# The row maximum of a full attention tile, taken in two parts on VectorE

## The reference, cut to what matters

```python
T, D, H, HD = 1250, 512, 8, 64
# spatial attention (KS_) and cross attention (KC_): every token sees every token
att = softmax(einsum('bthd,bshd->bhts', q, k), axis=-1)     # 1250 x 1250 for each head
o   = einsum('bhts,bshd->bthd', att, v)
# temporal attention (KT_): the same with a causal mask, row t sees columns 0..t
```

## Time and profile before

| | |
|---|---|
| median of 3 runs | 1983.16 us (1981.05 to 1983.17) |
| the profiled execution, its own time | 1988.85 us |
| its span in the profile | 1987.1 us |
| spatial attention, first maximum to last exponential | 516.9 to 821.5 us |
| causal attention | 1033.2 to 1249 us |
| cross attention | 1366.2 to 1671 us |
| busy over the span | PE 87%, DVE 60%, ACT 45%, POOL 35% |

### The profile page before, as it was taken

The page is one execution under the profiler, slowest core; times in us unless marked ns, Lnnn a source line. Parts: engine busy times, 40 slices in busy tenths (PEclk is TensorE's granted clock), DMA queues, the critical chain, the costliest instruction groups (busy, mean ns, idle before and its releaser), DMA issues.

```text
span 1987.1 us, 27321 instructions
## 1 busy us (share of the span) xinstructions
PE 1720.9 (87%) x9816; PEld 1411.9 (71%) x9816; DVE 1186.2 (60%) x2214; ACT 886.9 (45%) x1736; POOL 693.5 (35%) x448
## 2 busy tenths in 40 slices
PE   2776989859999999798977777699999998789998
PEld 1544876548788888676866666577888887568776
DVE  7998124630588888631057777515888886873333
ACT  3774321311477777512145665313777775321000
POOL 4021010033525424022346454135245337253331
PEclk9988999969999999898989999799999999889999
DMA  3000000132021111023311223011121130011111
GB/s 97 7 22 22 0 23 15 57 125 60 19 52 28 27 33 42 6 89 131 73 26 27 52 49 134 17 39 40 31 48 27 27 91 20 12 43 37 37 37 57
DMA packets 33003, 88.42 MB, mean 44 GB/s; under 512 B 5190, under 2 KB 5660, under 8 KB 32369
## 3 DMA queue, kind: packets, MB, share of 16 engines
q1 hardware_dynamic: 32881, 86.83, 16.2%
HBM read 43.29 MB, written 12.80 MB: 28 GB/s over the span
## 4 chain that ended last, share of the span: by engine, by line
PE 53%; DVE 25%; ACT 10%; issue 6%; DMA 2%; SPq 1%; POOL 1%; DVEq 1%; ACTq 0%; POOLq 0%
PE ps L568 10%; PE ps L569 10%; PE ps L570 10%; DVE ngm L1402 7%; PE ps L740 6%; ACT F L933 5%; PE ps L750 4%; PE ps L741 4%; DVE R L1411 4%; PE ps L767 3%; DVE F L1297 3%; ACT R L944 3%; PE ps L689 2%; DVE F L1423 2%; PE ps L786 2%
## 5 line engine op out<-in xcount | busy, mean ns | idle before, releaser
L438 POOL TENSOR_TENSOR w_hi<-w_raw,zero 128x512 fp32r<-128x512 f32 x96 | 109.5, 1141 | 803.2 <-PE ps L570 505.5
L944 ACT ACTIVATE R<-ps 125x500 fp32r<-125x500 f32 (+3 forms) x624 | 278.1, 513 | 243.3 <-PE ps L750 242.5
L1402 DVE TENSOR_REDUCE ngm<-ps 125x1 f32<-125x1250 f32 (+5 forms) x240 | 302.3, 1260 | 60.9 <-PE ps L741 55.9
L1411 DVE TENSOR_TENSOR R<-ps,R 125x500 fp32r<-125x500 f32 (+3 forms) x624 | 326.2, 574 | 17.4 <-ACT R L944 16.8
L740 PE MATMUL ps<-R 128*125 128x512 f32 (+4 forms) x624 | 258.9, 415 | 61.1 <-DVE R L1411 55.1
L933 ACT ACTIVATE F<-ps,ngm 125x1250 f32<-125x1250 f32 (+5 forms) x240 | 277.7, 1157 | 76.1 <-DVE ngm L1402 72.0
L767 PE MATMUL ps<-R 125*128 125x252 f32 (+1 forms) x2080 | 300.2, 289 | 8.7 <-DVE F L1423 7.9
L750 PE MATMUL ps<-ident,F 125*125 125x125 f32 x2040 | 270.9, 278 | 10.7 <-ACT F L933 10.7
L767 PEld LDWEIGHTS ps<-R 125*128 125x128 f32 x2080 | 261.0, 190 | 10.9 <-DVE R L1411 9.4
L750 PEld LDWEIGHTS ps<-ident,F 125*125 125x125 f32 x2040 | 249.6, 192 | 14.9 <-ACT F L933 12.9
L568 PE MATMUL ps<-R,w_hi 128*128 128x512 f32 (+1 forms) x576 | 213.8, 371 | 41.9 <-POOL w_lo L453 13.9
(11 more groups left out here) (172 smaller groups left out, 2478.0 us busy)
## 6 DMA issues: line engine op xcount, KB each, us to landing
R<-F SPq DMA_DIRECT2D x96, 312.5 KB, 5.2
w_raw<-in_weights SPq DMA_DIRECT2D x96, 256.0 KB, 2.7
TB<-in_x SPq DMA_DIRECT2D x10, 250.0 KB
x_d<-F SPq DMA_DIRECT2D x10, 250.0 KB
zt_d<-F SPq DMA_DIRECT2D x1, 2500.0 KB, 8.5
F<-zt_d SPq DMA_DIRECT2D x1, 2500.0 KB, 12.4
qc_d<-F SPq DMA_DIRECT2D x4, 625.0 KB, 3.9
xt_d<-F SPq DMA_DIRECT2D x4, 625.0 KB, 3.4
```

What stands on the lines that cost most here:

```text
L438: return eng.tensor_tensor(to, a, zero[0:to.shape[0], :].to_broadcast(list(to.shape)), ALU.add)
L944: eng.activation(PT[0][:, g % 2, 4 * bank:4 * bank + nb, n % 2, 0:P], ps[0:P, 3 * (n % 2) + bank, 0:P * nb].rearrange("p (c t) -> p c t", ...
L1402: eng.tensor_reduce(out=ngm[0:P, n % 2:n % 2 + 1], in_=flat(n % 2)[0:P, 0:K.cols[i]], op=ALU.max, axis=AX.X, negate=True).then_inc(A.negma ...
L1411: eng.tensor_tensor(PT[1][blk], ps[0:P, 3 * (n % 2) + bank, 0:P * nb].rearrange("p (c t) -> p c t", c=nb), PT[0][blk].bitcast(F32), ALU.su ...
```

## The change

In a full attention tile PE counts a new semaphore `A.early` up when the second bank of scores has landed. DVE then takes the maximum of columns 0 to 1023 as soon as that has come, the maximum of columns 1024 to 1249 when `A.scores` has come, and the smaller of the two negated values with a `tensor_tensor` of one column. Both reduces go through `link`. The causal attention keeps its code.

```diff
+        ngp = sb("ngp", [128, 2, 2])
...
-        A = Sems(sem, "att", "qin0 qin1 cut scores negmax exp tr hi lo pv inv ihi ilo bc bot post norm lk")
+        A = Sems(sem, "att", "qin0 qin1 cut early scores negmax exp tr hi lo pv inv ihi ilo bc bot post norm lk")
...
                     ins = eng.matmul(to, QSL[b][:, P * i:P * i + P], KS[b][:, lo:lo + w], start=False, stop=True)
+                    if c == 1 and not K.causal:
+                        ins.then_inc(A.early, 1)
                 ins.then_inc(A.scores, 1)
...
                 def greatest(c, hp, n):
+                    i = n % NT
+                    if not K.causal:
+                        t = 2 * NT * hp + n + (H * NT if K.turn else 0)
+                        eng.wait_ge(A.early, t + 1)
+                        c(eng.tensor_reduce(out=ngp[0:P, n % 2, 0:1], in_=flat(n % 2)[0:P, 0:1024], op=ALU.max,
+                                            axis=AX.X, negate=True))
+                        eng.wait_ge(A.scores, K.tile(hp, n))
+                        c(eng.tensor_reduce(out=ngp[0:P, n % 2, 1:2], in_=flat(n % 2)[0:P, 1024:T], op=ALU.max,
+                                            axis=AX.X, negate=True))
+                        eng.tensor_tensor(ngm[0:P, n % 2:n % 2 + 1], ngp[0:P, n % 2, 0:1], ngp[0:P, n % 2, 1:2], ALU.min
+                                          ).then_inc(A.negmax, 1)
+                        return
                     eng.wait_ge(A.scores, K.tile(hp, n))
-                    i = n % NT
```

## The result

The changed kernel takes 2074.82 us (median, 2068.95 to 2076.91) beside 1982.59 us before: 1.046 times as long, with a 95% interval of 1.044 to 1.048. The direction was as forecast, the size was not: 92 us instead of 26, far above the range. Its profiled execution has a span of 2075.1 us against 1987.1.

What follows compares the result with a forecast made beforehand. A chain of waits through DVE, PE and ACT, 7.54 us per two tiles, was taken as the bound, not PE. Per stage 9.5 + 3.0 + 0.4 = 12.9 us, for two +26: 1983.16 + 26 = 2009 us, range 1999 to 2025.

Steps and rivals of the forecast that it cites:

- the term of the minimum: One-column minimum after the two reduces on DVE: taken to last 0.15 us, the next instruction starting 0.07 after its start.
- What the split costs: Two reduces, links and minimum in place of one reduce on DVE: +0.38 us to `probs_lo` and to the end of `ngm`.
- The bound below: Least price of the minimum on DVE: not nothing, as no DVE row is under 0.13 us and starts are 0.07 apart.
- The odd tile: Odd-numbered tile's maximum, behind `output` on DVE: on the chain of waits, so each two-tile round takes 0.38 us more.
- The four rounds of a gap: Rounds where `spread_inverses` fills PE, three such stretches a stage: +1.0 us for each stretch, 3.0 us a stage.
- The margin of 0.07 for the even tile: Even tile's `ngm` ready at 571.60, ACT's exponential starting at 571.67: 0.07 us left, so no cost, narrowly.
- The price of a link: Chained DVE instruction starts 0.03 us after the previous end, an unchained one 0.08 before it: 0.11 us for each link.
- The rule that a semaphore costs nothing extra: Skill's rule, weighed and not followed: the split would cost 0.16 us a round, the sum near 9 us instead of 26.
- No change: Rival: PE is the bound after all, its slack absorbing DVE's extra work; time stays 1983 us; 4%.
- faster: Rival: the early start of the even tile's maximum decides; 16 us gained at no split cost, 1967 us; 3%.
- cheap links: Rival: a linked DVE instruction starts like one without a wait; split costs 0.16 us, 1992 us; 8%, up to 2001.
- The even tile comes onto the chain as well: Rival: minimum takes 0.30 us, even tile's `ngm` 0.08 too late, round grows by 0.61, 2026 us; 15% above 2018.

Runs made afterwards that it cites:

- the twin with the reduce: The changed kernel with the minimum of the two partial maxima taken by a tensor_reduce over two columns instead of a tensor_tensor: 2015.13 us, 1.0136 times the kernel before.
- even tiles only: The changed kernel with a tensor_reduce minimum and the split in even-numbered tiles alone, odd tiles keeping one reduce: 1986.45 us, 0.9995 times the kernel before.
- the run without the early start: The changed kernel with a tensor_reduce minimum and both partial reduces waiting for `A.scores`: 2023.61 us, 1.0197 times the kernel before.

## Why the prediction was wrong, and where it was right

**The step that failed** is the term of the minimum in the part "What the split costs": "the nearest is the one-element TENSOR_SCALAR of the router, 0.14 us ... I take 0.15 and 0.07, the row being of the same size", with an upper bound of 0.30 from L1401. It measured 0.525 on average, up to 2.345. I chose the row by size, and what mattered was its operands: the router's instruction has one tensor input, L1401 takes one of its two from PSUM, and the minimum reads two tensors from SBUF, where it waits for the running GpSimd instruction. Nothing in the prediction looked at GpSimd, whose work I had only named as "other queues". (The bound below, "no DVE row is under 0.13", was wrong too: the memsets of L1473 take 0.08. It changed nothing.) The trace of before did show the wait. At 1715 us, in the timeline of both engines, before:

```profile
1715.35 1.03 POOL L557 TENSOR_TENSOR R<-F,zero 128x500 fp32r<-128x500 f32 x1 [2.07 <-ACT F L1110]
1715.41 1.51 DVE L1529 TENSOR_TENSOR F<-F 125x512 f32<-125x512 f32 x1
```

L1529 adds two SBUF tiles of 512 columns; the shortest of its ten takes 0.69 us, this one 1.51, because it gets going only when L557 ends, at 1716.38. The Trainium skill states the rule ("SBUF — State Buffer", section "SBUF: two separate sides"): VectorE and GpSimd share one pair of SBUF ports as an exclusive lock that goes to whoever starts first, for a whole instruction. On VectorE an instruction with two SBUF inputs needs it while GpSimd reads SBUF, and one that runs in a two-port mode needs it too. The runs here agree on two inputs, with up to 2345 ns against at most 158 for the reduce with its one. (That the tensor_scalar of 200 columns ran in a two-port mode no run shows.) They agree on the other direction as well: L557 at 1711.81, behind an L1529 that had started at 1711.70, took 1.46 us instead of 1.03. "For a whole instruction" doesn't fit L487, which let the minimum through 0.77 us after its start of 2.07; there the measurement decides.

**What it added.** Of the 95 us in the two stages, 27 are the split itself (the twin with the reduce: 13.5 + 13.8; forecast 12.9 each). The minima's waits are 84.0 - 24.8 = 59 us. That leaves 9, and the two stages show a granted clock of 0.96 and 0.97 in place of 0.99. Two rounds of the changed kernel, from `output` to `output`, and the stretch of low clock in the second (length, busy time by engine, then the granted clock):

```profile
563.78:573.42 9.64, 7.53 (x54) 6.36 (x53) 8.64 (x13) 5.84 (x11) 8.60 (x4) 1.00 0.01 2
573.42:584.25 10.83, 8.75 (x53) 7.92 (x52) 8.89 (x14) 5.84 (x11) 6.17 (x4) 0.84 0.00 1
579.07:582.49 3.42, 3.42 (x17) 3.31 (x16) 2.65 (x5) 1.41 (x4) 0.97 (x1) 0.50 0.00 0
```

The first is 1.72 us longer than a round with a short minimum (7.92) and holds waits of 0.72 + 1.05 = 1.77 us: the waits pass into the round one to one. The second is 2.90 us longer with 1.83 us of waits (the minimum at 575.43). PE had been idle for 2.08 us up to 578.06, from 579.07 on its clock was at 0.50 (1.2 GHz), and ten transposes took 2.33 us where the usual is 1.26. Over 78 such rounds the waits are 48.9 us and the lengthening over the twin's rounds is 55.1. What lies between is in seven rounds with a granted clock of 0.83 to 0.85 and three right behind one of these (7.4 us together); no other round is more than 0.1 us longer than its waits. The remaining 13 us, 10 of them waits, lie in the first and last tiles of the stages. No run here holds the clock still, so that the low clock is the cause of the rest is read from the place where it lies.

**The rest of the working**, judged by the twin with the reduce, where the failed term is right: 28 us for 26. From the first reduce to `probs_lo` 1.76 for 1.75. Round 7.94 for 7.92, and 8.05 for 8.05 in second heads. The odd tile carries the whole cost and the even tile none: right (even tiles only: 0.9995). The four rounds of a gap are 1.1 us longer (31.15 to 32.25, in the second pair of heads) for 1.0. The margin of 0.07 for the even tile: about right, as the run without the early start shows, since 0.22 later made 0.15 of a round in second heads and 0.18 in first heads. The price of a link, 0.11: 0.12 measured. The rule that a semaphore costs nothing extra (the Trainium skill, "VectorE: DVE Perf Modes", "The DRAIN you can't avoid") doesn't hold for these reduces: 1.26 against 1.14 us from start to start.

**The rivals.** No change and faster fell, and so did cheap links, with 0.12 us for one. "The even tile comes onto the chain as well" came nearest, with a minimum dearer than taken, but it priced that at 0.30, without a wait for GpSimd, and so ended at 2026.

## What to carry to other kernels

Choose the row that prices a new instruction by its operands first and by its size second: where it reads from (SBUF or PSUM) and how many tensors. A VectorE instruction with two tensor inputs in SBUF, of one column even, can last as long as the GpSimd instruction that runs beside it; where GpSimd is busy, write a minimum of two columns as a reduce over them, or give one as a per-partition scalar, and look in the trace at the longest of a group and not only at the median. And this split paid only where its first part fell into idle time of the engine that carries the chain: with both parts behind `output` it cost 28 us, with the first part ahead of `output` it brought 18.

## What the runs showed of the hardware that I had not expected

A tensor_tensor of 125 x 1 with both inputs in SBUF took 0.16 to 2.35 us, and 52 of the 53 long ones ended within 0.06 us of a GpSimd instruction's end. The exception is a GpSimd tensor_scalar (L487): it held the minimum only in its first 0.77 of 2.07 us. With one input (tensor_reduce, 125 x 2) it took 0.154 to 0.158 us beside the same GpSimd work, and as a tensor_scalar with the second column as the scalar 0.212 to 0.219. A tensor_scalar of 200 bf16 columns, also with one tensor input, did wait for GpSimd: 0.27 us as a rule, up to 1.32 beside it.
